# Cross-attention and routed experts on one core: separate PSUM banks and an earlier projection for the last eight attention steps

## The reference

```
x = x + attention(layernorm(x), ctx, ctx, mask) @ W_out.T      # 16 heads of 32
xn = layernorm(x)
q = tanh(xn @ proj_w.T / 0.3);  logits = -(6 - q.anchors)/2 / temp   # 6 experts
weights = softmax over the 2 largest logits
x = x + sum over experts of weight * (gelu(xn @ w1[e]) @ w2[e])   # 512 -> 256 -> 512
```

## Time and profile before

| | us |
|---|---|
| median of 3 executions (648.66 to 651.44) | 650.73 |
| the profiled execution | 647.7 |
| its span, first to last instruction | 645.0 |
| TensorE, VectorE, ScalarE, GpSimd busy | 564.1, 423.5, 343.3, 300.1 |

### The profile page before, as it was taken

The page is one execution under the profiler, slowest core; times in us unless marked ns, Lnnn a source line. Parts: engine busy times, 40 slices in busy tenths (PEclk is TensorE's granted clock), DMA queues, the critical chain, the costliest instruction groups (busy, mean ns, idle before and its releaser), DMA issues.

```text
span 645.0 us, 14215 instructions
## 1 busy us (share of the span) xinstructions
PE 564.1 (87%) x4472; PEld 413.7 (64%) x4472; DVE 423.5 (66%) x895; ACT 343.3 (53%) x664; POOL 300.1 (47%) x434
## 2 busy tenths in 40 slices
PE   5678899999989899788879799998999999999950
PEld 3564355556556555444456788887999999888840
DVE  4667777667687867656989555576853357566653
ACT  3638875677758555565646364343345545444420
POOL 5434765656538665664758140404000056544443
PEclk9769999999999999999979699999999999999985
DMA  5321122222322338273447364658577789999986
GB/s 165 100 57 59 52 96 87 81 100 99 99 71 94 125 107 311 99 262 118 176 155 254 104 220 154 239 201 308 182 232 228 219 274 366 400 406 406 383 296 188
DMA packets 60274, 122.07 MB, mean 189 GB/s; under 512 B 7718, under 2 KB 10790, under 8 KB 60204
## 3 DMA queue, kind: packets, MB, share of 16 engines
q1 hardware_dynamic: 49964, 87.61, 40.2%
q0 software_dynamic: 10240, 33.56, 14.5%
HBM read 67.93 MB, written 53.22 MB: 188 GB/s over the span
## 4 chain that ended last, share of the span: by engine, by line
PE 60%; DVE 11%; DMA 11%; issue 8%; ACT 6%; POOL 2%; SPq 1%; POOLq 0%; DVEq 0%; ACTq 0%
DMA y_d<-ysb 10%; PE ps L1672 5%; PE ps L1523 4%; PE ps L1567 4%; PE ps L1544 4%; PE ps L1752 4%; PE ps L1754 4%; PE ps L1753 4%; PE ps L1778 3%; PE ps L1780 3%; PE ps L1779 3%; PE ps L1738 3%; PE ps L1568 3%; PE ps L1569 3%; PE ps L1697 3%
## 5 line engine op out<-in xcount | busy, mean ns | idle before, releaser
L798 POOL DMA_INDIRECT yg<-y_d,y_row x64 | 65.6, 1025 | 127.5 <-DMA y_d<-ysb 81.6
L728 POOL DMA_INDIRECT xs_d<-x,to_row x64 | 65.8, 1028 | 73.1 <-DVE to_row L1174 38.4
L919 ACT ACTIVATE prob<-ps 128x512 f32<-128x512 f32 x128 | 65.9, 601 | 60.5 <-PE ps L1547 60.5
L1092 DVE TENSOR_REDUCE nmax<-ps 128x4 f32<-128x512 f32 x128 | 79.5, 684 | 22.5 <-PE ps L1523 22.5
L1752 PE MATMUL ps<-w1H,xgH 128*128 x276 | 84.4, 306 | 5.6 <-DVE xgL L1407 5.0
L1407 DVE TENSOR_TENSOR xgL<-ps,xgH 128x512 fp32r<-128x512 f32 x69 | 47.5, 689 | 58.1 <-ACT xgH L1001 57.8
L1754 PE MATMUL ps<-w1L,xgH 128*128 x276 | 78.3, 284 | 0.0
L1753 PE MATMUL ps<-w1H,xgL 128*128 x276 | 78.2, 283 | 0.0
L758 POOL TENSOR_TENSOR atT<-less,raw 128x512 f32<-128x512 f32 x32 | 40.8, 1274 | 45.1 <-issue 39.0
L1778 PE MATMUL ps<-w2H,hH 128*128 x138 | 60.2, 436 | 0.8 <-DVE ysb L1420 0.8
L1021 ACT ACTIVATE ysb<-ps 128x512 f32<-128x512 f32 x43 | 25.7, 599 | 62.9 <-DMA y_d<-ysb 39.3
(11 more groups left out here) (214 smaller groups left out, 1268.9 us busy)
## 6 DMA issues: line engine op xcount, KB each, us to landing
xg<-xs_d SPq DMA_DIRECT2D x69, 256.0 KB, 3.7
y_d<-ysb SPq DMA_DIRECT2D x69, 256.0 KB, 3.2
xin<-in_x SPq DMA_DIRECT2D x32, 256.0 KB, 2.8
x<-in_x SPq DMA_DIRECT2D x32, 256.0 KB, 3.1
x_d<-x SPq DMA_DIRECT2D x32, 256.0 KB, 2.1
x2t<-x_d SPq DMA_DIRECT2D x32, 256.0 KB, 4.8
out_x<-x2t SPq DMA_DIRECT2D x32, 256.0 KB, 6.1
w1L<-in_L_ffn_w SPq DMA_DIRECT2D x6, 512.0 KB, 6.6
```

Of the source, the lines that this page charges most:

```text
L919: nc.scalar.activation(prob[v % 2][:, h, :], ps[:, B_SC + h, :], ACT.Exp, scale=scale).then_inc(exp_done, 1)
L1092: nc.vector.tensor_reduce(nmax[:, n % 2, :, g * hpg + h], ps[:, token_bank(h), :].rearrange("p (t k) -> p t k", t=4), axis=AX.X, op=ALU.ma ...
```

## The change

It touches only what runs from step 37 (`S_AFTER`, the first step with no scores by token) on.

- Turned rows from tile 15 on (`W_T2`) use bank 5, the projection from tile 20 on (`W_OUT`) bank 4. Neither waits for an exponential, and scores by key no longer wait for them: their two waits stop at the last tile that used banks 1 and 2.
- TensorE makes the projection right behind the turned rows, ahead of mask factors, sums and router. VectorE does the residual ahead of `newton`.
- `first_list` moves behind `newton`. The list is turned in bank 7, behind the last `newton`.
- Block 7's projection waits bank by bank.
- The last two of the 12 lower halves move from behind the last residual to expert slots 2 and 3, behind these slots' `xgL`.

```diff
-        B_LIST = 5
+        B_LIST = 7
+
+        A_OUT, A_T2 = 4, 5
 
         def out_bank(n, t):
-            return I_OUT if n < INSIDE else B_OUT + t
+            if n < INSIDE:
+                return I_OUT if 4 * n + t < W_OUT else A_OUT
+            return B_OUT + t
-        def t2_bank(n):
-            return I_T2 if n + 1 < INSIDE else B_LATE
+        def t2_bank(n, t):
+            if n + 1 < INSIDE:
+                return I_T2 if 4 * n + t < W_T2 else A_T2
+            return B_LATE
...
+        S_AFTER = L_TOK + ntile
+        W_OUT, W_T2 = S_AFTER - L_MID, S_AFTER - L_MID - 4 - L_T2
...
-        LOWER_LAST = [w_all[4:6], w_all[6:8], w_all[8:10], w_all[10:12]]
+        LOWER_LAST = [w_all[4:6], w_all[6:8], w_all[8:10], ()]
+        LOWER_SLOT = {2: w_all[10:11], 3: w_all[11:12]}
...
-                if (i, q) == (blk_per_batch + 2, 0):
-                    first_list()
+                tail = s >= S_AFTER
+                if tail:
+                    residual(i, q)
 
                 d = s - L_PV
                 if live(d, ntile):
...
+                if (i, q) == (blk_per_batch + 2, 0):
+                    first_list()
...
-                if i >= 0:
+                if i >= 0 and not tail:
                     residual(i, q)
...
+                    for e in LOWER_SLOT.get(TPI * i + k, ()):
+                        lower(*e)
...
-                after(pe, t2_done, rows_turned(v + L_KEY)[0])
-                after(pe, add_done, v + L_KEY - L_MID)
+                after(pe, t2_done, min(rows_turned(v + L_KEY)[0], W_T2))
+                after(pe, add_done, min(v + L_KEY - L_MID, W_OUT))
...
-                        pe.wait_ge(add_done, 4 * n)
-                        pe.wait_ge(t2_done, 4 * (n - 1))
+                    elif t == I_T2:
+                        pe.wait_ge(t2_done, W_T2)
+                    elif t == I_OUT:
+                        pe.wait_ge(add_done, W_OUT)
+                    elif t == I_Z:
                         pe.wait_ge(used_done, n - 2)
...
+                tail = s >= S_AFTER
+                if tail:
+                    pe.wait_ge(mx_done, hpg * ntile)
                 if live(w, ntile):
-                    unit_left(I_T2 + 1)
+                    if not tail:
+                        unit_left(I_T2 + 1)
                     rows_transposed(w // 4, w % 4)
+                if tail:
+                    project(i, q)
...
-                if i >= 0:
+                if i >= 0 and not tail:
                     unit_left(I_OUT + 1)
                     project(i, q)
...
                 if s == S_LAST - 1:
-                    pe.wait_ge(mx_done, hpg * ntile)
+                    pe.wait_ge(newton_done, ntile)
                     turn_list(B_LIST, 1)
```

More of the change, by code:

```diff
@@ L869, in rows_out @@
                     nc.scalar.activation(x2T[:, t, :, :],
-                                         ps[:, t2_bank(n), :].rearrange("p (k t) -> p k t", k=kchunks), ACT.Copy)\
+                                         ps[:, t2_bank(n, t), :].rearrange("p (k t) -> p k t", k=kchunks), ACT.Copy)\
                       .then_inc(t2_done, 1)
@@ L1580, in rows_transposed @@
                     for c in range(kchunks):
-                        last = nc.tensor.transpose(ps[:, t2_bank(n), c * P:(c + 1) * P], x2[:, n % 4, t, c * P:(c + 1) * P],
+                        last = nc.tensor.transpose(ps[:, t2_bank(n, t), c * P:(c + 1) * P], x2[:, n % 4, t, c * P:(c + 1) * P],
                                                    ident[:])
```

## The result

The change takes 640.05 us (median of 4, 639.05 to 641.37) beside 651.05 for the kernel before (median of 4, the three shown ahead and one more): ratio 0.9843, interval 0.981 to 0.9876. The profiled execution of the change took 639.05, its span is 636.2.

A forecast was written before the change was run, and what follows sets the result against it. VectorE was taken as fullest until the first expert tile, TensorE behind it. Terms 3.2 - 1.3 + 2.5 + 1.0 = 5.4 us gave 645.3 for the median (642.3 for an execution like the profiled one), range 641.3 to 649.6.

The forecast's parts named there:

- steps 37 to 40: Scores to scores over four steps: 36.6 us before, 33.45 after, a gain of 3.2 us (between 2.5 and 3.8).
- the hand-over: Last residuals to first expert tiles: two lower halves moved to slots 2 and 3 gain 1.0 us (ends 0 and 1.3).
- the clock: TensorE's granted clock, 0.50 from 353 to 365 us: up to 2 us gained or 1.5 lost, taken as 0.
- VectorE's holes and stretched ones, steps 41 to 44: VectorE from scores of step 41: holes net -1.3 us, fewer stretched instructions +2.5 us.
- The step forecast at 7.8: Step 37 (q = 0): 5.0 us, then mask factors 0.66, sums 0.99, PV 0.99 and 0.2 of issue.
- The two pieces behind VectorE and ScalarE: Steps 38 and 40: next scores wait for ScalarE's router copy (4.0 us from the sums' start) and VectorE's `used` (3.45).
- New holes: VectorE, steps 41 to 44: waits of 1.8 at residual (6,0), 0.9 at newton, 1.5 at residual (6,2); together 4.2 us.
- Stretched ones: VectorE operations lengthened beside GpSimd products, step 41 to 330 us: 7.3 us over short forms; saving taken 2.5, ends 0 and 5.
- old holes: VectorE waits that go: 2.41 ahead of residual (6,3), 0.2 at squash, 0.3 of residual (5,3); together 2.9 us.
- three to four stretched ones left: VectorE between scores of step 41 and the choices: seven stretched before, three to four after, about 3.5 us, saving 3.8.
- VectorE hands it back: Stretched VectorE instructions just move to other neighbours, holes remain: gain 2.4 us, 648.3; chance 0.12.
- The end is set by DMA: DMA engines, full at 550 to 600 us, wait off the early start: 1 us left, 649.7; chance 0.04.

The follow-up runs named there:

- the banks alone: The change with both orders old (projection behind sums and router part, residual behind router and choices), keeping new banks, list and slots: ratio 0.9895 to the kernel before.
- the kernel with the gates later: The change with shares and gates of steps 38 and 42 moved behind residual and newton: ratio 0.9823 to the kernel before.
- the change again: The changed kernel, unedited, run again beside later versions on one chip: median 639.27 us against 647.63 before, ratio 0.9859.
- filler: Matmuls of no use in TensorE's hand-over waits: 16 on the kernel before, ratio 0.9898; 18 on the change, 635.99 us, ratio 0.9822.
- projection late: The change with TensorE's projection back at its old place, behind sums and router part, in its new bank: ratio 1.0103 to the kernel before.
- last projection early: The kernel before with only projection (6,3) of step 44 moved ahead of the prefix: ratio 1.0004.
- without slots: The change with all twelve lower halves made before the expert slots again: ratio 0.9876 to the kernel before.

## Why the prediction was right and wrong

**Which steps failed.** The direction was right, and so was most of the mechanism; sizes were off. Two terms of the sum were too small: steps 37 to 40 (3.2 us, and 4.9 in every execution with both new orders), and the hand-over with the clock set to 0 (1.0 + 0, and 3.8 in the first profile, 1.6 in the second). And the 3.0 us by which the profiled execution of before lay under its median were added to the forecast, where the profiled execution of the change lay 1.0 under its own. What the sum put at nothing, the stretch behind tile 3, took 3.4 back in the first profile and 3.2 in the second.

**The account of the miss.** 645.3 less 640.05 is 5.25 us. For an execution like the profiled one the forecast was 642.3, and 639.05 came: 3.25. Of these, 1.29 lie ahead of step 37, where nothing was changed (267.03 against 268.32), and 2.1 are the terms below (7.5 gained from 37 to the end, against 5.4); around the span lie 2.85 us and not 2.7, which takes 0.15 off. The other 2.0 are the offset: the profiled execution of before lay 3.0 under the median shown, that of the change 1.0 under its own, and the prediction had carried the 3.0 over.

| term | forecast | first profile | again |
|---|---|---|---|
| steps 37 to 40 | 3.2 | 4.9 | 4.9 |
| VectorE's holes and stretched ones, steps 41 to 44 | −1.3 + 2.5 = 1.2 | 2.2 | 0.6 |
| last residual to tile 3: slots and clock | 1.0 + 0 | 3.8 | 1.6 |
| tile 3 to the end | 0 | −3.4 | −3.2 |
| sum (of unrounded terms) | 5.4 | 7.5 | 4.0 |

**Steps 37 to 40: mechanism right, size too small, and the one term that is the same in every run.** Which steps would end on what was right for all four. The step forecast at 7.8 took 6.94. From the start of one piece to the start of the next, turned rows took 0.41 us where 0.66 was put in, mask factors 0.53 and not 0.66, sums 0.88 and not 0.99, projection 2.84 ahead of the mask factors (2.93 or 2.94 ahead of the sums in the three other steps) and not 2.95, and there was no issue gap. The 0.66 are the length of the row, which reaches into the next piece: in the change the row of 268.34 is 0.66 long too. The rest depends on what comes next. Two pairs of the kernel before, neither with a wait ahead of the second piece:

```profile
272.45 1.06 PE L1672 MATMUL ps<-prob,ones 128*32 128x512 f32 x8
273.44 0.50 PE L1567 MATMUL ps<-woH,atH 128*128 128x512 f32 x1
...
280.56 1.06 PE L1672 MATMUL ps<-prob,ones 128*32 128x512 f32 x8
281.44 1.04 PE L1594 MATMUL ps<-x2T,projT 128*32 128x512 f32 x8
```

The same sums take 0.99 us ahead of the projection and 0.88 ahead of the router part; in the change they take 0.88 ahead of the router part and PV, and 1.00 ahead of the logits (287.44 to 288.44), which were forecast at 0.81 and took 0.99. Turned rows take 0.58 or 0.59 ahead of the sums in the steps 38 to 41 of before and, with no wait ahead of them, with the banks alone; ahead of the projection they take 0.38 to 0.41 in the change, with a wait (306.57) or without. So the new order changed the lengths of the pieces, and rows of the old order could not give all of them. The upper end given for the term does not come out either: turned rows at 0.6 instead of 0.66 are 0.24 us over four steps, which makes 3.4 and not 3.8, and 4.9 lay beyond both. The two pieces behind VectorE and ScalarE came as forecast (sums to scores 4.16 against 4.1, 3.66 against 3.55).

What the prediction did not see is why it needs both orders. It gave the gain to the banks, which end the 1.12 us of waiting in each step, and took the order as what goes with it; the banks alone give 1.2 of 4.9.

**Steps 41 to 44.** New holes 1.28, 0.83, 1.26 and 0.36 make 3.7 against the 4.2 forecast; the long old one is gone as forecast. Stretched ones: by the rows above, zero_row twice, wgt, pwgt and the first pair of lower halves are some 4.0 us over their short forms (0.17, 0.17, 0.18, 0.21, 2.34), against 7.3 before: 3.3 saved, between the 2.5 taken and the whole 3.8. With the 2.9 of old holes that makes 2.5 by this count, and 2.2 were measured. The count of "three to four stretched ones left" was right, of small ones; the pair of lower halves is a fifth. That it is alignment, and was not to be had by moving the gates alone, the kernel with the gates later shows. The same stretch in the change again gave only 0.6, through the clock.

**Hand-over.** From the last residual to the first low half it is 1.69 us and not 3.93: the two lower halves. Prefix against last residual gained 1.5, forecast 1.3 at most. The third up-projection, at 353.40, is 11.0 us earlier from 37 than at 365.67 before, though the prefix is only 8.6 earlier: the other 2.4 lie between the prefix and that up-projection (3.12 us at clock 1.00, where it was 5.53 at 0.50), and are put down to the clock, which the prediction named as worth up to 2 and then set to 0. That was the second term that was mis-sized. Slots and clock are hard to part: with the slots the stretch never took over 12.48 us, without them and without filler never under 13.70.

**The rivals.** "VectorE hands it back" by 2.4 instead of 5.4 fell. "The end is set by DMA" fell too: the stretch from tile 45 on is 120.0 and 119.7 us in the two kernels that start it latest (projection late, last projection early), as long as in those that start it early; that of the execution of before was a short one. The 1.8 us that the first profile lost between tiles 3 and 45 stay open. Its clock was 0.62 from 433 to 437.5 us, behind waits of 1.00, 0.54 and 1.40 around the second list; but without slots and with the projection late the same three waits stand there at a clock of 1.00, and the stretch is nearly as long (161.0 and 160.4 against 161.5), so the clock is not the whole of it, and DMA is not ruled out there. These five kernels take 160.4 to 162.2 us there and the nine other executions 159.2 to 159.8, the change again among them. The slower rival, the clock falling before projection (6,2), had its place right and was seen once, in the change again: one projection at half clock costs 1.6 us, not the two or three at 2.2 from which it would have decided.

**What stays open.** The ratios give a gain of about 9 to 10 us, the two profiles 7.5 and 4.0 from 37 on. The second is its kernel's slowest execution; the first had 1.3 more ahead of step 37, and the kernel before was profiled in an execution 3.4 under its median of 651.05. Whether its usual executions lose those 3 us in the edited stretch or elsewhere isn't known: only one of them has a trace. The clock has a part in it, as in the change again (0.955 in its slowest execution, 0.963 to 0.968 in the others), but a part of unknown size. Nor is it shown what decides whether the clock comes back after the first or the third up-projection.

## What to carry to other kernels

When a buffer is freed so that work can be moved up, look at the next user of the shared resource: here the wait moved to it until the moved work was long enough to cover it. Where producer and consumer share one buffer on two in-order engines, try both orders in one edit: here either one alone was slower than neither. Price a piece from its start to the start of the next, by a row that has the same next piece behind it. And where a wait stands in front of a stretch at half clock, count both as one term, with the clock's share in the range rather than at 0.

## What was not expected of the hardware

- The time from one group of matmuls to the next depends on what the next one is. Eight sums (128x32, 512 columns) take 0.85 to 0.89 us ahead of the router part or PV (128x32 too) and 0.99 to 1.00 ahead of the projection, the logits or the prefix (128x128), with a wait ahead of them or without: so at all 103 such places from 240 to 312 us of the fourteen profiles. Four transposes take 0.58 or 0.59 us ahead of the sums in steps 38 to 41 of the kernel before and 0.38 to 0.41 ahead of the projection in steps 37 to 41 of the change.
- Sixteen matmuls whose result nobody reads made the kernel before 1% faster (0.9898). Its profile has a granted clock of 1.00 from 350 to 362 us, where it was 0.50 from 353 to 365, and 2.7 us less in that stretch; the rest of the 1% stands in no profile.
- The same kernel with the same waits (1.25 and 1.26 us) ahead of the same projection ran it at full clock in one execution and at half clock in another, and its executions reach from 637.1 to 643.9 us.
